# Repeated matmuls on the tensor engine in the waits of a four-stage convolution and attention kernel

## The chip, the cores and the metric

One core of a Trainium2 chip runs the whole kernel. The metric is the device time of one execution in microseconds; the median of three runs of the kernel before is 1879.36 us (1878.1 to 1879.47).

## The reference, cut to what matters

The input is x of 8 images, 64 channels, 56 by 56 pixels. Four residual blocks follow one another, each on a group-normalised x (32 groups of 2 channels, over all pixels of an image):

```python
x = x + _L0_conv_ref(_gn(x), ...)   # dynamic 3x3 filter: per channel cf times per pixel sf, 9 taps summed
x = x + _L1_conv_ref(_gn(x), ...)   # v * sigmoid(q . mean of k): two 64x64 products and a gate
x = x + _L2_conv_ref(_gn(x), ...)   # 3x3 convolution, 64 to 64 channels, weights -1, 0 or 1
x = x + _L3_conv_ref(_gn(x), ...)   # attention over all 3136 pixels: softmax(Q K) V, dk 16, dv 64
```

The mean and the variance of a group need the whole picture, so no stage can begin before the stage ahead of it has ended.

## The kernel before, in words

Two images lie side by side on the 128 partitions (64 channels each). So there are 4 groups of two images, worked off one after the other by `group(g, more)` on every engine; the first three in a loop, the last one unrolled behind it. A picture of 3136 pixels is cut into 7 chunks (NJ) of 448 pixels (CH, 8 rows). PSUM has 8 banks, PS[:, 0] to PS[:, 7]; `small` is bank 7, where the one-column results of the statistics go.

On the tensor engine a group runs as follows, in program order (nothing but this order and the semaphore waits sets when an instruction runs):

- The filter taps of block 0 (`taps`, L1085 and L1093), until the sums are in xw.
- `pair_stats(1)` (L1113, its two parts L1038 and L1042): DVE has gathered mean and variance per channel; a matmul by `pair` averages the means of the two channels of a group (`pair_mean`), DVE forms the squared difference, a second matmul averages that (`pair_var`), DVE adds epsilon (L483), POOL takes the power -0.5 (L954), DVE forms the bias (L487), and ACT normalises chunk by chunk (L777).
- For block 1 the engine then multiplies the pooled mean by wk (L1115), waits for DVE, multiplies by wq and half8 (L1117, L1118), waits until DVE has built U (L616), and does 7 times two fp32 matmuls of 448 columns (L1126, L1127).
- `pair_stats(2)` (L1130), and the convolution: per chunk 18 matmuls (L1135), the first of which waits until ACT has normalised two chunks.
- `pair_stats(3)` (L1145), and the 7 products with the joined weights of Q and K (L1148). ACT and DVE split them into three bf16 parts, and SP's DMAs spread them into Qa and Ka.
- The first maxima. `tile_of(bank, s, b, t)` (L1160 to L1164) is two matmuls of 64 output partitions and 448 columns each, one for each image (so a tile is a pair of matmuls). For the first superblock 49 tiles (TILES) are written to banks 0 to 6 in turn in the order FIRST_ORDER; DVE takes the maximum of each row (L672), and for the rows of three of the seven blocks ACT then sums the exponentials (L854). The tile that follows in the same bank waits for that (`first_used`, `first_summed`). Between them `value_columns` (L1156) makes the transposed values.
- DVE splits the maxima into bf16 parts (`split_max`, L679 to L688, `negm`). PE transposes these (`max_rows`, L1188), ACT copies them into Qa (L869, `mrow`), and only then can the scores begin (L1195).
- 7 superblocks of 25 steps each: scores (L1195), exponentials on ACT (L897), values (L1239), and the maxima of the next superblock (L1163 again, with L665 on DVE). In the last superblock of a group the front of the next group (statistics and filters of block 0) is laid between; these waits call `pair_mean` and `pair_var` themselves and not `pair_stats`.

The places that the change and the prediction touch are the two lines of `pair_stats`, the lines behind L1115 and L1118, and the loop L1273 to L1288.

Of the kernel before, what the change touches and what calls it, by code (L numbers as in the profile page):

```python
# [25 lines left out]
CH = ROWS * W  # L26
NJ = HW // CH
# [13 lines left out]
PITCH = 32  # L41
# [9 lines left out]
TILES = NJ * NJ  # L51
# [32 lines left out]
def order_first():  # L84

    blocks = [b for b in range(ACT_BLOCKS, NJ)]
    summed = {m * NJ // ACT_BLOCKS: m for m in range(ACT_BLOCKS)}
    row = [summed[n] if n in summed else blocks.pop(0) for n in range(NJ)]
    return [(b, t) for t in range(NJ) for b in row]


FIRST_ORDER = order_first()
# [76 lines left out]
def build(nc, x, weights, vectors, cst, out):  # L169
    with ExitStack() as ctx:  # L170
        def sb(name, shape, dt=F32):
            return ctx.enter_context(nc.sbuf_tensor(name, shape, dt))
# [15 lines left out]
        selb = sb("selb", [3 * PITCH, TAPS, P], BF16)  # L188
        identb = sb("identb", [P, P], BF16)
# [55 lines left out]
        PS = ctx.enter_context(nc.psum_tensor("PS", [P, 8, 512], F32))  # L245
# [8 lines left out]
        def pad_rows(t, r0, n, c0=0):  # L254

            return t[:, r0 * PW + c0:(r0 + n) * PW + c0].rearrange("p (r w) -> p r w", w=PW)[:, :, 0:W]
# [7 lines left out]
        def wcol(name):  # L264
            return wz[:, COLS[name][0]:COLS[name][1]]
# [761 lines left out]
        def _(pe):  # L1027
            mm = nc.tensor.matmul
# [7 lines left out]
            def pair_mean(g, layer, bank):  # L1036
                pe.wait_ge(gn_mean[layer], g + 1)
                mm(bank[:, 0:1], pair, mv[:, 0:1], start=True, stop=True).then_inc(gn_pm[layer], 1)  # L1038

            def pair_var(g, layer, bank):  # L1040
                pe.wait_ge(gn_sq[layer], g + 1)
                mm(bank[:, 1:2], pair, sq[:, :], start=True, stop=True).then_inc(gn_pv[layer], 1)  # L1042
# [31 lines left out]
                last.then_inc(sft_ready, 1)  # L1074

            def group(g, more):
                def pair_stats(layer):
                    pair_mean(g, layer, small)
                    pair_var(g, layer, small)

                def spread_tap(j, t):

                    k = NJ * g + j
                    pe.wait_ge(prod_ready, TAPS * k + t + 1)
                    mm(PS[:, t % TAP_BANKS, 0:CH], selb[:, t, :], SF[:, ds(j * CH, CH)],  # L1085
                       start=True, stop=True).then_inc(tap_ready, 1)
# [23 lines left out]
                add_tap(NJ - 1, 0, TAPS - 1)  # L1110


                pair_stats(1)  # L1113
                pe.wait_ge(pooled_ready, 2 * g + 2)
                mm(small[0:2 * CR, 20:21], wcol("wk"), pooled[:, 1:2], start=True, stop=True).then_inc(km_ps, 1)  # L1115
                pe.wait_ge(km_ready, g + 1)
                mm(small[:, 21:22], wcol("wq")[0:2 * CR], km[:, 0:1], start=True, stop=True)  # L1117
                mm(small[:, 22:23], half8[0:2 * CR], km[:, 1:2], start=True, stop=True).then_inc(u_ps, 1)  # L1118
                for j in range(NJ):
                    pe.wait_ge(xn_ready[1], NJ * g + j + 1)  # L1120
                    if j == 0:
                        pe.wait_ge(U_ready, g + 1)
                    if j >= 3:
                        pe.wait_ge(gated_ready, NJ * g + j - 2)
                    xnj = pad_rows(xnp, ROWS * j + 1, ROWS, 1)
                    mm(PS[:, j % 3, 0:CH], wcol("wv"), xnj, start=True, stop=True)  # L1126
                    mm(PS[:, 3 + j % 3, 0:CH], U[:, :], xnj, start=True, stop=True).then_inc(l1_ps, 1)  # L1127


                pair_stats(2)  # L1130
                def convolve(j, need):
                    for src, ready in ((xh, xh_ready), (xl, xl_ready)):
                        pe.wait_ge(ready, NJ * g + need)
                        for t in range(TAPS):
                            last = mm(PS[:, j, 0:CH], wt[:, t * P:(t + 1) * P],  # L1135
                                      pad_rows_at(src, j * (ROWS * PW) + (t // 3) * PW + t % 3, ROWS),
                                      start=(src is xh and t == 0), stop=(src is xl and t == TAPS - 1))
                    last.then_inc(conv_ready, 1)
# [3 lines left out]
                convolve(NJ - 1, NJ)  # L1142


                pair_stats(3)  # L1145
                for j in range(NJ):
                    pe.wait_ge(xn_ready[3], NJ * g + j + 1)
                    mm(PS[0:4 * DK, j, 0:CH], wcol("qk3"), xnf[:, j * CH:(j + 1) * CH],  # L1148
                       start=True, stop=True).then_inc(qk_ps, 1)
                def value_columns(i):  # L1150

                    if i:
                        pe.wait_ge(v_ready, NJ * g + i)
                    for j in range(4 * i, min(4 * i + 4, NQ)):
                        r = key_rows(j)
                        last = mm(PS[0:r, 7, (j % 4) * P:(j % 4 + 1) * P], xnf[:, j * QC:j * QC + r], wcol("wv3"),  # L1156
                                  start=True, stop=True)
                    last.then_inc(v_ps, 1)

                def tile_of(bank, s, b, t):  # L1160

                    for h in range(2):
                        last = mm(PS[C * h:C * h + C, bank, 0:CH], Qa[0:KROWS, h, s * CH + b * C:s * CH + b * C + C],  # L1163
                                  Ka[0:KROWS, h, t * CH:(t + 1) * CH], start=True, stop=True)  # L1164
                    return last
# [17 lines left out]
                def max_rows(sidx, bank):  # L1183

                    rowb = PS[:, bank, :].bitcast(BF16)
                    pe.wait_ge(negm, sidx + 1)
                    for b in range(NJ):
                        last = nc.tensor.transpose(rowb[KROWS:KROWS + 3, b * BLK:(b + 1) * BLK], mp[:, b, :], identb[:, :])  # L1188
                    last.then_inc(mrow_ps, 1)
# [80 lines left out]

                pe.wait_ge(q_first, 16 * (SPREADS * (g + 1) + 1))
                pe.wait_ge(k_first, 16 * (SPREADS * (g + 1) + 1))
                for i in range(TILES):  # L1273
                    b, t = FIRST_ORDER[i]
                    if i < NJ:
                        pe.wait_ge(rest_h, NJ * g + i + 1)
                    elif FIRST_ORDER[i - NJ][0] < ACT_BLOCKS:
                        pe.wait_ge(first_summed, ACT_TILES * g + sum(b < ACT_BLOCKS for b, _ in FIRST_ORDER[:i - NJ + 1]))
                    else:
                        pe.wait_ge(first_used, TILES * g + i - NJ + 1)  # L1280
                    if i == FIRST_KEYS * NJ:
                        pe.wait_ge(k_rest, 16 * (SPREADS * (g + 1) + 1))
                    tile_of(i % NJ, 0, b, t).then_inc(first_ready, 1)
                    if i % NJ == NJ // 2:
                        value_columns(i // NJ)
                pe.wait_ge(v_ready, NJ * (g + 1))
                max_rows(NJ * g, 7)
                pe.wait_ge(mrow, NJ * g + 1)  # L1288
                pe.wait_ge(q_rest, 16 * (SPREADS * (g + 1) + 1))
                for j in range(2):  # L1290
# [17 lines left out]
            with pe.Fori(0, GROUPS - 1) as g:  # L1308
                group(g, True)
            group(GROUPS - 1, False)  # L1310


# [64 lines left out]
```

## Time and profile before

| what | value |
|---|---|
| median of three runs | 1879.36 us |
| the profiled execution | 1879.96 us, of which the trace spans 1878.2 us |
| PE busy | 1646.5 us (88%) |
| DVE, ACT, POOL busy | 1258.0, 1249.8, 1099.3 us |
| mean granted clock of TensorE | 0.950 |

All times in the trace count from the start of its span. In a row, a bracket at the end says how long the engine was idle before the row and who released it. In a row of windows "(x12)" is the number of instructions, and PEclk is the granted clock of TensorE over the window: 1.00 is 2.4 GHz, 0.50 is 1.2 GHz, and a value between says that the window holds some of both. A group of two images takes some 460 us. The waits at issue lie in its first 150 us, and the first group's are shown in most rows.

### The profile page before, as it was taken

To read this page: it belongs to the slowest core of one execution; us is meant where nothing else is said; L and a number is where in the kernel's file an instruction comes from. 1 tells how busy PE (TensorE), PEld (TensorE's weight loads), DVE (VectorE), ACT (ScalarE), POOL (GpSimd) and SP (SyncE) were. 2 spreads that over 40 slices of the span, in tenths; PEclk is the share of its full clock that TensorE was granted. 3 is DMA by queue.
4 is the path that set the end of the run, shared out by engine and by line. 5 is a ranking of instruction groups with operands and counts; after the bars stand their busy time and mean duration, and the time that the engine had idled before them with its cause. 6 is when DMAs were issued, how large, how long until landed. Compare 5 with 4: busy or idle time off the path is not lost.

```text
span 1878.2 us, 35981 instructions
## 1 busy us (share of the span) xinstructions
PE 1646.5 (88%) x10840; PEld 826.0 (44%) x10840; DVE 1258.0 (67%) x2446; ACT 1249.8 (67%) x2324; POOL 1099.3 (59%) x898
## 2 busy tenths in 40 slices
PE   5887899999887699999988779999999787999997
PEld 4363344444436344444444534444454353444442
DVE  5947777775584777777467477777748657777760
ACT  2036788888412788888831278888872347888885
POOL 3610577778651067777855006777777402677777
PEclk9988899999889899999998889999999898999998
DMA  2004000000000400000000040000000011000000
GB/s 84 0 1 86 2 7 6 6 6 7 11 0 1 86 1 6 6 6 7 11 7 1 1 85 1 6 6 11 6 6 6 0 27 26 6 6 6 6 6 11
DMA packets 10104, 26.91 MB, mean 14 GB/s; under 512 B 2256, under 2 KB 6608, under 8 KB 9424
## 3 DMA queue, kind: packets, MB, share of 16 engines
q1 hardware_dynamic: 9936, 24.79, 5.5%
q8 instruction: 90, 1.47, 0.3%
q14 instruction: 78, 0.64, 0.1%
HBM read 8.73 MB, written 6.42 MB: 8 GB/s over the span
## 4 chain that ended last, share of the span: by engine, by line
PE 54%; issue 15%; DVE 12%; POOL 9%; ACT 9%; POOLq 1%; DVEq 0%; ACTq 0%
PE PS L1239 22%; PE PS L1163 11%; PE PS L1195 10%; DVE nmt L672 4%; ACT PS L854 3%; DVE nmt L665 2%; ACT Pb L897 2%; PE PS L1060 2%; POOL VT L970 2%; POOL VT L965 2%; PE PS L1135 2%; POOL VT L967 2%; POOL VT L974 1%; POOL accP L1008 1%; PE PS L1126 1%
## 5 line engine op out<-in xcount | busy, mean ns | idle before, releaser
L665 DVE TENSOR_REDUCE nmt<-PS 128x1 f32<-128x448 f32 x1176 | 680.3, 620 | 280.8 <-PE PS L1163 276.4
L1008 POOL TENSOR_TENSOR accP<-accP,Pb 128x512 f32<-128x512 f32 (+1 forms) x532 | 678.3, 1275 | 168.1 <-ACT Pb L897 144.6
L897 ACT ACTIVATE Pb<-PS 128x896 f32<-128x896 f32 (+1 forms) x700 | 638.9, 914 | 130.2 <-PE PS L1195 107.9
L1239 PE MATMUL PS<-Pb,VT 128*64 128x448 f32 x2800 | 656.0, 548 | 4.4 <-ACT Pb L897 3.6
L1163 PE MATMUL PS<-Ka,Qa 96*64 96x448 bf16 x2744 | 480.9, 362 | 55.9 <-DVE nmt L665 28.1
L1195 PE MATMUL PS<-Qa,Ka 99*64 99x448 bf16 x2744 | 489.8, 358 | 5.3 <-ACT Qa L869 4.0
L854 ACT ACTIVATE PS<-PS,nmt 128x448 f32<-128x448 f32 x588 | 356.3, 606 | 56.8 <-DVE nmt L672 29.4
L1163 PEld LDWEIGHTS PS<-Ka,Qa 96*64 96x64 bf16 x2744 | 159.4, 111 | 324.3 <-issue 127.2
L1195 PEld LDWEIGHTS PS<-Qa,Ka 99*64 99x64 bf16 x2744 | 162.3, 111 | 248.8 <-issue 184.3
L1239 PEld LDWEIGHTS PS<-Pb,VT 128*64 128x64 f32 x2800 | 191.6, 138 | 96.2 <-ACT Pb L897 24.5
L777 ACT ACTIVATE xnp<-xw,nb,rstd 128x448 f32<-128x448 f32 x56 | 40.5, 750 | 204.9 <-DVE nb L487 204.9
L1001 POOL TENSOR_TENSOR accQ<-Pb 128x512 f32<-128x512 f32 x28 | 35.6, 1271 | 234.2 <-ACT Pb L897 234.2
L579 DVE SCALAR_TENSOR_TENSOR Pb<-PS,cf,xnp 128x448 f32<-128x448 f32 x252 | 154.9, 677 | 17.1 <-PE PS L1085 13.4
L1093 PE MATMUL PS<-Pb,cs 128*128 128x448 f32 x280 | 135.5, 566 | 0.7 <-DVE Pb L579 0.7
L1008 POOL TENSOR_TENSOR accQ<-accQ,Pb 128x512 f32<-128x512 f32 x84 | 106.7, 1270 | 46.2 <-ACT Pb L897 44.9
L854 ACT ACTIVATION_READ_ACCUMULATOR PS<-PS,nmt 128x1 f32 x588 | 116.0, 197 | 0.0
L954 POOL TENSOR_TENSOR rstd<-ve,mhalf 128x1 f32<-128x1 f32 x16 | 8.8, 550 | 172.0 <-DVE ve L483 172.0
L672 DVE TENSOR_REDUCE nmt<-PS 128x1 f32<-128x448 f32 x196 | 104.8, 613 | 1.7 <-PE PS L1163 1.7
L1085 PE MATMUL PS<-xnf,selb 96*128 (+1 forms) x252 | 84.9, 376 | 13.3 <-issue 6.2
L777 ACT ACTIVATE xnf<-xw,nb,rstd 128x448 f32<-128x448 f32 x28 | 20.7, 752 | 102.8 <-DVE nb L487 102.8
L1135 PE MATMUL PS<-xh,wt 128*128 (+1 forms) x252 | 64.3, 404 | 10.6 <-ACT xh L777 10.6
L1085 PEld LDWEIGHTS PS<-xnf,selb 96*128 96x128 bf16 x252 | 25.0, 99 | 90.5 <-DVE Pb L579 50.7
(141 smaller groups left out, 1435.0 us busy)
## 6 DMA issues: line engine op xcount, KB each, us to landing
xin<-in_x SPq DMA_DIRECT2D x4, 1568.0 KB, 12.2
out<-xw SPq DMA_DIRECT2D x28, 224.0 KB, 1.9
Qa<-parts SPq DMA_DIRECT2D x24, 168.0 KB, 6.9
Ka<-parts SPq DMA_DIRECT2D x24, 112.0 KB, 3.8
Ka<-parts SPq DMA_DIRECT2D x24, 84.0 KB, 2.6
wz<-in_weights SPq DMA_DIRECT2D x1, 829.0 KB, 8.2
Qa<-parts SPq DMA_DIRECT2D x24, 28.0 KB, 1.9
cs<-in_cst SPq DMA_DIRECT2D x1, 576.0 KB, 8.8
```

The source lines that it names most:

```text
L579: nc.vector.scalar_tensor_tensor(out=rows(prod[:, t, :]), in0=rows(PS[:, t % TAP_BANKS, 0:CH]), scalar=cf[:, t:t + 1], in1=pad_rows_at(xnp ...
L665: nc.vector.reduce_max(nmt[:, target % 2, b, t:t + 1], PS[0:BLK, bank, 0:CH], X, negate=True).then_inc(mx_free, 1)
L672: nc.vector.reduce_max(nmt[:, 0, b, t:t + 1], PS[0:BLK, i % NJ, 0:CH], X, negate=True).then_inc(first_used, 1)
L854: return nc.scalar.activation(PS[0:BLK, bank, 0:CH], PS[0:BLK, bank, 0:CH], ACT.Exp, bias=nmt[:, target % 2, b, t:t + 1], accum_out=sm[:, ...
L897: nc.scalar.activation(Pb[0:r, j % PSLOTS, :, :], PS[0:r, 2 * (k % 2):2 * (k % 2) + 2, 0:CH], ACT.Exp).then_inc(exp_done, 1)
L1008: nc.gpsimd.tensor_tensor((accQ if j < TO_ACCP else accP)[0:r, :, REST:CH], (accQ if j <= TO_ACCP else accP)[0:r, :, REST:CH], Pb[0:r, j % ...
L1085: mm(PS[:, t % TAP_BANKS, 0:CH], selb[:, t, :], SF[:, ds(j * CH, CH)], start=True, stop=True).then_inc(tap_ready, 1)
L1093: mm(PS[:, ACCB + odd, 0:CH], identf, prod[:, t, :], start=(t == 0), stop=(t == TAPS - 1)).then_inc(tap_added, 1)
L1135: last = mm(PS[:, j, 0:CH], wt[:, t * P:(t + 1) * P], pad_rows_at(src, j * (ROWS * PW) + (t // 3) * PW + t % 3, ROWS), start=(src is xh an ...
L1163: last = mm(PS[C * h:C * h + C, bank, 0:CH], Qa[0:KROWS, h, s * CH + b * C:s * CH + b * C + C], Ka[0:KROWS, h, t * CH:(t + 1) * CH], start ...
L1195: ins = mm(PS[c:c + C, 2 * (k % 2) + h, 0:CH], Ka[0:KROWS + 3, h, j * QC + c:j * QC + c + C], Qa[0:KROWS + 3, h, s * CH:(s + 1) * CH], sta ...
L1239: last = mm(PS[C * h:C * h + C, OB, 0:CH], VT[:, j, C * h:C * h + C], Pb[:, j % PSLOTS, h, :], start=(j == 0), stop=(j == NQ - 1))
```

## The change

`pair_stats` gets a second argument, and a new function `keep_busy(n)` issues n matmuls of 96 rows, 128 output partitions and 448 columns in bf16 on constants, into bank 6. One stands between `pair_mean` and `pair_var` at each of the three places; behind `pair_var` stand 2, 6 and 5. Two more places in block 1 get 1 and 2. The loop over the first maxima goes on for 7 more turns, in each of which the engine waits until the bank is free and then issues a last tile again twice (its result is overwritten later and never read), and 4 more such tiles stand behind `max_rows`. No other engine's program changes.

```diff
             def group(g, more):
-                def pair_stats(layer):
+                def keep_busy(n):
+
+                    for _ in range(n):
+                        mm(PS[:, 6, 0:CH], identb[0:3 * PITCH, :],
+                           selb[:, :, :].rearrange("p t c -> p (t c)")[:, 0:CH], start=True, stop=True)
+
+                def pair_stats(layer, meanwhile):
                     pair_mean(g, layer, small)
+                    keep_busy(1)
                     pair_var(g, layer, small)
+                    keep_busy(meanwhile)
...
-                pair_stats(1)
+                pair_stats(1, 2)
                 pe.wait_ge(pooled_ready, 2 * g + 2)
                 mm(small[0:2 * CR, 20:21], wcol("wk"), pooled[:, 1:2], start=True, stop=True).then_inc(km_ps, 1)
+                keep_busy(1)
                 pe.wait_ge(km_ready, g + 1)
                 mm(small[:, 21:22], wcol("wq")[0:2 * CR], km[:, 0:1], start=True, stop=True)
                 mm(small[:, 22:23], half8[0:2 * CR], km[:, 1:2], start=True, stop=True).then_inc(u_ps, 1)
+                keep_busy(2)
...
-                pair_stats(2)
+                pair_stats(2, 6)
...
-                pair_stats(3)
+                pair_stats(3, 5)
...
-                for i in range(TILES):
-                    b, t = FIRST_ORDER[i]
+                for i in range(TILES + NJ):
                     if i < NJ:
                         pe.wait_ge(rest_h, NJ * g + i + 1)
                     elif FIRST_ORDER[i - NJ][0] < ACT_BLOCKS:
                         pe.wait_ge(first_summed, ACT_TILES * g + sum(b < ACT_BLOCKS for b, _ in FIRST_ORDER[:i - NJ + 1]))
                     else:
                         pe.wait_ge(first_used, TILES * g + i - NJ + 1)
+                    if i >= TILES:
+                        for _ in range(2):
+                            tile_of(i % NJ, 0, NJ - 1, NJ - 1)
+                        continue
+                    b, t = FIRST_ORDER[i]
...
                 max_rows(NJ * g, 7)
+                for _ in range(4):
+                    tile_of(NJ - 1, 0, NJ - 1, NJ - 1)
                 pe.wait_ge(mrow, NJ * g + 1)
```

## Rows read from the trace of the kernel before

**Rows 1.** The page: engine shares, and TensorE's clock in 40 slices
```profile
PE 1646.5 (88%) x10840; PEld 826.0 (44%) x10840; DVE 1258.0 (67%) x2446; ACT 1249.8 (67%) x2324; POOL 1099.3 (59%) x898
...
PEclk9988899999889899999998889999999898999998
```
**Rows 2.** Windows: start:end and length us, each engine's busy us, PEclk, DMA
```profile
90.98:96.10 5.12, 2.39 (x10) 2.08 (x11) 1.50 (x9) 2.39 (x4) 0.55 (x1) 0.50 0.01 2
96.10:99.72 3.62, 3.62 (x5) 1.82 (x6) 0.00 (x0) 0.58 (x2) 0.00 (x0) 0.50 0.00 0
116.47:120.20 3.73, 3.73 (x10) 3.34 (x11) 1.88 (x3) 3.73 (x7) 0.00 (x0) 0.50 0.02 4
```
**Rows 3.** Timeline, what ends each wait: start, length us, engine, line
```profile
93.79 0.21 PE L1115 MATMUL PS<-pooled,wz 128*16 128x1 f32 x2 [1.14 <-DVE pooled L610]
94.43 0.58 PE L1117 MATMUL PS<-km,wz 16*128 16x1 f32 x2 [0.42 <-DVE km L613]
96.10 1.83 PE L1126 MATMUL PS<-xnp,wz 128*128 128x448 f32 x2 [0.67 <-DVE U L616]
97.73 1.70 PE L1127 MATMUL PS<-xnp,U 128*128 128x448 f32 x2
97.73 0.34 PEld L1127 LDWEIGHTS PS<-xnp,U 128*128 128x128 f32 x1 [0.41 <-issue]
116.47 3.72 PE L1135 MATMUL PS<-xh,wt 128*128 x9 [2.65 <-ACT xh L777]
150.67 4.29 PE L1148 MATMUL PS<-xnf,wz 128*64 128x448 f32 x6 [2.10 <-ACT xnf L777]
```
**Rows 4.** Timeline, from the last first maxima to the first scores
```profile
183.41 6.99 DVE L672 TENSOR_REDUCE nmt<-PS 128x1 f32<-128x448 f32 x13
187.19 0.73 PE L1163 MATMUL PS<-Ka,Qa 96*64 96x448 bf16 x5
191.19 0.18 DVE L688 TENSOR_REDUCE mp<-nm 128x7 bf16<-128x21 f32 x1
191.51 0.91 PE L1188 MATMUL PS<-identb,mp 128*3 128x128 bf16 x7 [3.59 <-DVE mp L688]
192.46 0.91 ACT L869 ACTIVATE Qa<-PS 3x896 bf16<-3x896 bf16 x1 [2.20 <-PE PS L1188]
193.42 1.70 PE L1195 MATMUL PS<-Qa,Ka 99*64 99x448 bf16 x8 [1.00 <-ACT Qa L869]
```
**Rows 5.** Windows around the same place, in all four groups
```profile
172.00:187.90 15.90, 11.93 (x96) 7.12 (x96) 15.90 (x31) 11.30 (x30) 0.00 (x0) 1.00 0.54 131
187.95:191.50 3.55, 0.00 (x0) 0.01 (x1) 3.32 (x11) 1.63 (x6) 0.00 (x0) 0.57 0.00 0
191.50:198.70 7.20, 5.84 (x29) 2.62 (x31) 1.78 (x3) 4.98 (x10) 1.97 (x2) 0.50 0.01 2
652.50:662.92 10.42, 9.08 (x43) 3.94 (x45) 2.39 (x4) 5.58 (x12) 2.53 (x2) 0.50 0.01 2
1116.11:1123.72 7.61, 6.27 (x31) 2.85 (x33) 1.78 (x3) 5.41 (x11) 2.39 (x2) 0.50 0.01 2
1573.40:1581.10 7.70, 6.43 (x31) 2.83 (x33) 1.78 (x3) 5.46 (x11) 2.53 (x2) 0.50 0.01 3
656.46:659.50 3.04, 3.04 (x14) 1.44 (x16) 1.78 (x3) 2.91 (x8) 1.78 (x2) 0.50 0.00 0
168.00:171.40 3.40, 3.40 (x20) 2.20 (x21) 2.87 (x7) 2.07 (x6) 0.00 (x0) 0.50 1.07 127
```
**Rows 6.** Timeline: neighbouring pairs of 448 columns at either clock
```profile
195.47 0.59 PE L1195 MATMUL PS<-Qa,Ka 99*64 99x448 bf16 x2 [0.35 <-ACT Pb L897]
195.84 0.59 PE L1163 MATMUL PS<-Ka,Qa 96*64 96x448 bf16 x2
...
199.53 0.36 PE L1195 MATMUL PS<-Qa,Ka 99*64 99x448 bf16 x2
199.72 0.36 PE L1163 MATMUL PS<-Ka,Qa 96*64 96x448 bf16 x2
```

## The prediction

> **What bounds the kernel now.** I read the page first. PE is busy 88% of the span and the other engines 67% or less, so PE is the engine to look at; but its clock is at tenths of 8 and 9 in a good part of the slices [rows 1]. The mean granted clock is 0.950; with two levels, 1.00 and 0.50, that is 10% of the span, some 188 us, at 1.2 GHz. A slow clock costs only where PE itself is what the others wait for, and then half of the busy time in it. So the second look is at windows cut at the waits, with the clock in them, and the third at the timeline inside.
>
> In each group the clock falls in the same places. Around the first statistics it is 0.50 from the pair mean at 90.98, with PE busy 2.39 of 5.12 us on one-column matmuls and weight loads, and it stays there over the next 3.62 us of unbroken fp32 work [rows 2]. At the second statistics PE waits 2.65 us for ACT, and then convolves 3.73 us at 0.50 [rows 2, 3]. At the third it waits 2.10 us [rows 3]. The costliest place is the end of the first maxima: PE does nothing from 187.95 to 191.50, the clock falls in it (mean 0.57), and the 7.20 us that follow run at 0.50 [rows 5]. All this lies on the path: the next stage cannot begin before a mean, a maximum or the split of it is there.
>
> What makes the clock return is seen in the same rows: each time PE had worked without a break for over 3 us (96.10 to 99.72, 116.47 to 120.20). 3.04 us without a break, from 656.46, were not enough, and the clock stayed at half until 662.92 [rows 2, 5].
>
> What keeps it up is seen from 172.00 to 187.90: PE busy 11.93 of 15.90 us, with a break in each row of tiles, and the clock stayed at 1.00 throughout [rows 5].
>
> **The repeats behind the first maxima.** A tile is one pair of 448-column matmuls. Pairs start 0.37 us apart at 0.50 (195.47, 195.84) and 0.19 us apart at 1.00 (199.53, 199.72) [rows 6]. The change adds 7 x 2 = 14 pairs before `max_rows`: 2.6 us at the full clock, 5.2 us at half. DVE's maxima come every 6.99 / 13 = 0.54 us and end at 183.41 + 6.99 = 190.40; each frees a bank for two pairs (0.37 us). So at the full clock PE keeps pace with DVE, and the last two pairs end near 190.45 + 0.75 = 191.2 at the latest. The split maxima come at 191.19 + 0.18 = 191.37 and PE's transposes began at 191.51 [rows 4]. Nothing is late: the added work lies under DVE's maxima and splits, and costs 0. If the clock has fallen first, 14 pairs from 187.95 end at 193.1, 1.6 us late, less if it returns on the way.
>
> Behind `max_rows` come 4 pairs, 0.75 us at full clock and 1.5 us at half, in the 1.00 us in which PE waits for ACT's copy (0.91 us) [rows 4]: cost 0, or 0.5 us at half clock.
>
> Does the clock stay? PE worked until 187.19 + 0.73 = 187.9 [rows 4]. The repeats begin at about 188.0, the first bank being free, and from there to 191.2 PE has 2.6 us of work in 3.3, about the share that held the clock from 172.00 to 187.90. After that come the transposes, the 4 pairs and the scores; the thinnest place is from the scores to the end of the first exponential, under 1 us. I take it as staying up, with one group in four where it falls all the same, since the last row of tiles has a break just before 187.
>
> What is then saved is half of the busy time that PE now has at 0.50: 5.84, 9.08, 6.27 and 6.43 us in the four groups [rows 5], together 27.6, half 13.8 us. That it is PE that ends the steps there: of the 7.20 us it is busy 5.84, and the rest is the ACT copy and the first exponential, which do not get faster. The half holds for streaming and less for the fixed part of each. For this and for the one group in four in which the clock falls or the repeats come late by up to 1.6 us, I take off 1.5: -12.3 us. Bounds: 0 (the clock falls anyway) and -13.8.
>
> **keep_busy.** It is one matmul of 448 columns in bf16, so by the pairs 0.19 or 0.37 us, and here the clock is mostly at half already when it begins.
> - First statistics. The clock has fallen before the pair mean, where no repeat is; nothing is saved until it returns. The repeats are 1, 2, 1, 2 in waits of 0.50 (L1042, as long as the rows' others of this kind), 1.14, 0.42 and 0.67 us [rows 3]: 0.37, 0.75, 0.37 and 0.75 us at half clock. The last is 0.08 us too long, the one at L1117 leaves 0.05. PE still pauses between them, so the clock returns when it does now, after some 3.5 us of the fp32 work from 96.10. Value taken: +0.1 us a group. Bounds: +0.5 (one 0.37 us matmul more than a wait holds, and a bit) and -1.8 (half of the 3.62 us).
> - Second statistics. 6 x 0.37 = 2.2 us stand in 2.65 us [rows 3]. That leaves 0.4 us of pause ahead of the convolution. If it counts as a break, the clock returns 3.7 us into the convolution as now; if not, up to 2.6 us sooner, worth 1.3 us. Value taken: 0. Bounds: +0.1 and -1.9 a group (half of 3.73).
> - Third statistics. 5 x 0.37 = 1.9 us in 2.10 us. The six matmuls from 150.67 take 4.29 us, so the first product (two of them) takes 1.4 us where 0.7 would do [rows 3]; ACT waits for that one alone, since then it has more to do than PE. Value 0, bounds +0.1 and -0.7.
>
> These three give +0.4 us over four groups, with bounds of +2.8 and -17.6.
>
> The Trainium skill speaks against these repeats: TensorE: Matmul & The Clock Gate, Part 3, "The mechanism", has it that a weight load goes beside a running matmul only where the row groups differ. By that rule each fp32 weight load behind a repeat would wait for its end; an estimate from this and the loads' 0.34 us at half clock is three loads in the first statistics and one in each other one, up to 5 x 0.34 x 4 = 6.8 us, and the sum would be -5 us. The trace does not agree: the L1127 load of 0.34 us, on all 128 rows, begins at 97.73, while PE is busy without a break from 96.10 to 99.72 with matmuls on all rows [rows 2, 3]. So I leave it at the sum above.
>
> **Sum.** -12.3 + 0.4 = -11.9. The profiled execution took 1879.96 us (its span 1878.2 and 1.8 around it); this gives 1868.1. The median of the runs is 0.6 lower: 1867.5 us. What is late next in the freed place is ACT's exponential and then PE at its full speed.
>
> **The rivals.**
> 1. The clock also returns sooner, or from the first matmul, in the stages behind the statistics. For it: the repeats turn waits of 2.65 and 2.10 us into almost unbroken work. Against: the pauses left are 0.2 to 0.4 us, and unbroken work of 3.04 us was not enough [rows 5]. Price: half of 3.73 and half of 3.62 us and 0.7 us a group, four times 4.4 = 17.6 at most; I take 15 of it: 1852 us.
> 2. The clock falls all the same behind the maxima or in the copy of `max_rows`, and what is saved in one step is paid in the next. For it: the break before 187, the transposes, which are short, and ACT's 0.91 us. Against: the share of work above. Price: some 3 of the 13.8 us remain: 1876 us, and within 0.2% of before.
> 3. Slower. The clock falls at about 188.5 as now and the repeats run at half clock: they end 1.6 us late, the 4 behind `max_rows` 0.5 us late, and the clock is not given back before the scores; +2.1 us a group, +8.4, with +2.8 from the statistics at their upper bounds: 1891 us. It decides if a repeat on half the output columns does nothing for the clock. Against it: from 168.00 to 171.40, at 0.50, PE did just such tiles and value columns without a break, and from 172.00 it is at 1.00 [rows 5]. 14 pairs at half clock are themselves such a stretch.
> 4. The change does not do what it says: the repeats leave clock and times as they are. That would be 1880 us; rival 2 holds this chance.
>
> The Trainium skill, in the same page, Part 4, has a rule for rival 2: a transpose does not count as PE activity as another matmul does. No row cited here shows it; the 0.91 us of transposes would then be a pause.
>
> **How the numbers follow.** The forecast, the maxima alone: 0.57. Rival 1: 0.17. Rival 2 with 4: 0.16. Rival 3: 0.10. A change under 0.2% (3.8 us) can't be told from none. Faster by more than that: 0.57 + 0.17 and a part of rival 2, 0.06: 0.80. Within: 0.11 (the rest of rival 2 and a mild rival 3). Slower: 0.09. The range goes down to rival 1, with 1851, and up to 1878 through rival 2.
>
> **What would show it.** In the profile after, the stretch from the last maximum to the third exponential at 1.00 in most groups, the transposes starting no later behind L688 than 0.14 us, and scores 0.19 us apart. The convolution's and L1126's first 3.5 us still at 0.50. Mean clock up from 0.950 to about 0.965. The forecast is wrong if the clock is at 0.50 behind the repeats, if the transposes start late, or if the first fp32 products of a stage run at 1.00.

## The result and the profile after

The changed kernel takes 1865.64 us (median of four runs, 1865.11 to 1866.51) against 1879.41 us of the kernel before (1878.1 to 1880.94): the ratio is 0.9928 with a 95% interval of 0.9913 to 0.9944. The forecast was 1867.5 us. The profiled executions are 1866.14 us and 1879.96 us, so 13.8 us less.

The page of the changed kernel, its engine shares and the clock in 40 slices, beside [rows 1]:

```profile
PE 1674.4 (90%) x11060; PEld 831.4 (45%) x11060; DVE 1258.4 (67%) x2446; ACT 1248.1 (67%) x2324; POOL 1096.4 (59%) x898
...
PEclk9988999999889899999989899999999899999999
```

PE has 220 matmul records more and is busy 28 us longer, in a shorter span; the other engines do what they did. The mean granted clock went from 0.950 to 0.964.

The timeline from the last row of tiles to the first scores answers to [rows 4] (line numbers are 10 higher behind the change: L1173 is the tile, L1198 the transposes, L1205 the scores):

```profile
186.36 4.29 PE L1173 MATMUL PS<-Ka,Qa 96*64 96x448 bf16 x33
...
190.36 0.18 DVE L688 TENSOR_REDUCE mp<-nm 128x7 bf16<-128x21 f32 x1
...
190.69 0.55 PE L1198 MATMUL PS<-identb,mp 128*3 128x128 bf16 x7
191.17 0.95 PE L1173 MATMUL PS<-Ka,Qa 96*64 96x448 bf16 x8
191.28 0.91 ACT L869 ACTIVATE Qa<-PS 3x896 bf16<-3x896 bf16 x1 [1.85 <-PE PS L1198]
192.24 0.95 PE L1205 MATMUL PS<-Qa,Ka 99*64 99x448 bf16 x8
```

The 14 repeated pairs run on from the last real ones and end at 190.65. The last split maximum ends at 190.54 and the transposes begin 0.15 us later, where it was 0.14 before. They take 0.55 us and not 0.91, and the scores 0.95 and not 1.70.

The windows of the changed kernel: a stretch of each statistics and what follows, the repeats, and then, in each of the four groups, from the first transpose to the start of the sixth exponential (columns as in [rows 2]):

```profile
90.69:95.40 4.71, 4.05 (x16) 1.99 (x17) 1.50 (x9) 2.39 (x4) 0.55 (x1) 0.62 0.01 2
95.40:98.68 3.28, 3.28 (x6) 1.64 (x6) 0.00 (x0) 0.32 (x1) 0.00 (x0) 0.50 0.00 0
115.64:119.16 3.52, 3.52 (x10) 3.13 (x11) 1.88 (x3) 3.52 (x6) 0.00 (x0) 0.50 0.00 0
149.75:153.30 3.55, 3.55 (x5) 1.03 (x6) 0.62 (x1) 2.05 (x4) 0.00 (x0) 0.50 0.00 0
186.36:190.65 4.29, 3.95 (x36) 1.55 (x32) 4.08 (x13) 2.33 (x7) 0.00 (x0) 1.00 0.02 4
190.69:200.09 9.40, 8.57 (x73) 4.17 (x75) 3.74 (x7) 7.67 (x15) 4.05 (x4) 1.00 0.00 2
650.83:660.23 9.40, 8.57 (x73) 4.19 (x75) 3.74 (x7) 7.67 (x15) 4.04 (x4) 1.00 0.00 1
1108.36:1117.77 9.41, 8.58 (x73) 4.20 (x75) 3.75 (x7) 7.67 (x16) 4.05 (x4) 1.00 0.00 1
1562.32:1571.56 9.24, 8.49 (x73) 4.09 (x75) 3.66 (x7) 7.59 (x15) 4.05 (x4) 1.00 0.01 3
```

The same four stretches of the kernel before, first transpose to sixth exponential:

```profile
191.51:203.24 11.73, 10.38 (x65) 4.80 (x67) 3.84 (x7) 7.86 (x16) 4.06 (x4) 0.69 0.01 3
652.50:665.81 13.31, 11.97 (x65) 5.32 (x67) 3.93 (x7) 7.97 (x15) 4.06 (x4) 0.61 0.01 2
1116.11:1128.04 11.93, 10.59 (x65) 4.90 (x67) 3.84 (x7) 7.87 (x16) 4.05 (x4) 0.68 0.01 2
1573.40:1585.26 11.86, 10.59 (x65) 4.80 (x67) 3.76 (x7) 7.91 (x16) 4.05 (x4) 0.68 0.01 2
```

Read the length and PEclk. Before, 48.83 us at 0.61 to 0.69; after, 37.45 us at 1.00 in every group. That is 11.4 of the 13.8 us. The other 2.4 us are spread over all stretches; the largest piece, 1.2 us in the sum of the four groups, lies between the first pair mean and the second. In the stages behind the statistics the first 3.3 to 3.6 us still run at 0.50, in the convolution and in the Q and K products as in the fp32 work of block 1.

### The profile page after: what moved, and what is told of

Same layout as the page of the kernel before. It is cut to its first block, busy times and chain, and to the rows that moved or that the text cites. A ratio compares the mean times of both kernels' runs of the same rounds, so it can differ in the third digit from the quotient of the medians.

```text
span 1864.3 us, 36442 instructions
## 1 busy us (share of the span) xinstructions
PE 1674.4 (90%) x11060; PEld 831.4 (45%) x11060; DVE 1258.4 (67%) x2446; ACT 1248.1 (67%) x2324; POOL 1096.4 (59%) x898
## 4 chain that ended last, share of the span: by engine, by line
PE 52%; issue 15%; DVE 12%; POOL 10%; ACT 9%; POOLq 1%; DVEq 0%; ACTq 0%
PE PS L1249 21%; PE PS L1173 11%; PE PS L1205 10%; DVE nmt L672 4%; ACT PS L854 3%; ACT Pb L897 3%; DVE nmt L665 3%; POOL accP L1008 2%; POOL VT L965 2%; POOL VT L970 2%; POOL VT L967 2%; PE PS L1060 2%; PE PS L1145 2%; POOL VT L974 1%; PE PS L1136 1%
## 5 line engine op out<-in xcount | busy, mean ns | idle before, releaser
L1173 PE MATMUL PS<-Ka,Qa 96*64 96x448 bf16 x2888 | 493.6, 359 | 57.0 <-DVE nmt L665 28.1
L1205 PE MATMUL PS<-Qa,Ka 99*64 99x448 bf16 x2744 | 485.0, 354 | 3.3 <-ACT Pb L897 2.8
L1173 PEld LDWEIGHTS PS<-Ka,Qa 96*64 96x64 bf16 x2888 | 164.8, 110 | 332.5 <-issue 123.2
L1205 PEld LDWEIGHTS PS<-Qa,Ka 99*64 99x64 bf16 x2744 | 161.0, 110 | 245.6 <-issue 182.9
L579 DVE SCALAR_TENSOR_TENSOR Pb<-PS,cf,xnp 128x448 f32<-128x448 f32 x252 | 154.7, 677 | 15.3 <-PE PS L1093 13.8
L1093 PE MATMUL PS<-xnf,selb 96*128 (+1 forms) x252 | 83.6, 370 | 13.8 <-issue 6.9
## 6 DMA issues: line engine op xcount, KB each, us to landing
xin<-in_x SPq DMA_DIRECT2D x4, 1568.0 KB, 11.8
```

What stands on the lines that cost most here:

```text
L579: nc.vector.scalar_tensor_tensor(out=rows(prod[:, t, :]), in0=rows(PS[:, t % TAP_BANKS, 0:CH]), scalar=cf[:, t:t + 1], in1=pad_rows_at(xnp ...
L1205: ins = mm(PS[c:c + C, 2 * (k % 2) + h, 0:CH], Ka[0:KROWS + 3, h, j * QC + c:j * QC + c + C], Qa[0:KROWS + 3, h, s * CH:(s + 1) * CH], sta ...
```

## The experiments

My theory: the gain is the clock behind the first maxima, and keep_busy gives almost nothing, because the clock has fallen before it begins (that reason holds in part only, see below). The rival: keep_busy carries a good part. All ratios are to the kernel before on the same chip.

**maxima_only**, without keep_busy:

```diff
-                    keep_busy(1)
                     pair_var(g, layer, small)
-                    keep_busy(meanwhile)
```

and without the two calls in block 1.

> Only the repeats behind the first maxima (7 x 2 tiles and the 4 behind max_rows); no keep_busy. My theory, that these carry the gain and keep_busy nearly none: 1866 to 1868 us. If keep_busy carried the gain: 1877 to 1880 us. From the comparison of the traces of before and after (in the first fp32 stage the sum of four groups is 1.2 us shorter, from the last split maximum to the sixth exponential 11.3 us) I expect 1867 us.

1867.74 us, ratio 0.9951 (0.9937 to 0.9964).

**statistics_only**, keep_busy alone:

```diff
-                for i in range(TILES + NJ):
+                for i in range(TILES):
...
-                for _ in range(4):
-                    tile_of(NJ - 1, 0, NJ - 1, NJ - 1)
```

> Only keep_busy at the three statistics and in block 1; nothing behind the maxima. My theory: 1878 to 1880 us, the same as before within 0.2%, since a clock that has fallen before the mean returns only after unbroken work. The rival, that the clock returns sooner in these stages: 1872 us or less.

1877.26 us, ratio 0.9998 (0.9989 to 1.0007). keep_busy as it stands gives nothing that can be measured, and costs nothing. That the whole is 2 us faster than maxima_only may be chance: the two intervals overlap. In the profile of the whole, the stretch from the first pair mean to the second is 0.6 and 0.8 us shorter in two groups, 0.2 shorter in one and 0.4 longer in one. In the sum of the groups this stretch takes 84.5 us there, 85.7 us before, and 86.5 us in maxima_only and in statistics_only alike, so it does not follow keep_busy alone.

**fourteen_only** and **four_only** take the repeats behind the maxima apart; neither has keep_busy.

```diff
 # fourteen_only
-                for _ in range(4):
-                    tile_of(NJ - 1, 0, NJ - 1, NJ - 1)
 # four_only
-                for i in range(TILES + NJ):
+                for i in range(TILES):
```

> Only the 7 x 2 tiles between the last first maximum and max_rows; neither the 4 tiles behind max_rows nor keep_busy. If the clock is held up by the 14 tiles and the 4 are not needed: 1867 us and clock 1.00 up to the third exponential. If the wait for ACT's copy (1.0 us), with few matmuls on either side of it, lets the clock fall: in some groups 0.50 again behind the scores, 1868 to 1874 us.

> Only the 4 tiles behind max_rows. By my theory the clock has fallen by then, the 4 tiles take 1.5 us at half clock in a wait of 1.0 us and delay the scores by up to 0.5 us a group, and may bring the clock back one step sooner: 1875 to 1881 us. If they alone gave the gain: 1867 us.

fourteen_only: 1871.98 us, ratio 0.9971 (0.9962 to 0.9980); four_only: 1877.56 us, 1.0004 (0.9994 to 1.0013). The 4 are nothing by themselves. Without them the 14 give less by the medians, 1871.98 us against 1867.74 us of maxima_only on the same chip; the two intervals just touch, but every run of fourteen_only (1870.03 to 1875.86) is slower than every run of maxima_only (1867.66 to 1868.21). In fourteen_only's timeline of the second group PE waits 1.00 us for the copy and 0.71 us for the exponential, and the clock falls at 653.82:

```profile
650.08 0.55 PE L1194 MATMUL PS<-identb,mp 128*3 128x128 bf16 x7
651.63 0.95 PE L1201 MATMUL PS<-Qa,Ka 99*64 99x448 bf16 x8 [1.00 <-ACT Qa L869]
653.29 0.38 PE L1201 MATMUL PS<-Qa,Ka 99*64 99x448 bf16 x2 [0.71 <-ACT Pb L897]
...
654.68 2.95 PE L1245 MATMUL PS<-Pb,VT 128*64 128x448 f32 x8
```

Its window shows the half clock:

```profile
653.82:657.24 3.42, 3.42 (x16) 1.28 (x12) 1.78 (x3) 2.82 (x9) 2.53 (x2) 0.50 0.00 0
```

The 8 value matmuls take 2.95 us, where the changed kernel's take 1.67 us in the first group. The third group has such a fall too, the first and the last have none: this is rival 2's mechanism, in half of the groups.

**one_tile_a_turn**, **four_tiles_a_turn** and **transposes_a_turn** change only what each of the 7 turns does:

```diff
-                        for _ in range(2):
+                        for _ in range(1):    # one_tile_a_turn; range(4) in four_tiles_a_turn
                             tile_of(i % NJ, 0, NJ - 1, NJ - 1)
...
-                        for _ in range(2):    # transposes_a_turn
-                            tile_of(i % NJ, 0, NJ - 1, NJ - 1)
+                        for _ in range(7):
+                            nc.tensor.transpose(PS[:, i % NJ, :].bitcast(BF16)[:, 0:P], identb[:, :], identb[:, :])
```

> As the changed kernel, but each of the 7 turns issues one tile and not two. PE is then busy 0.19 of each 0.54 us between DVE's maxima. If what counts is that there is no pause longer than about half a microsecond: 1866 us, as with two. If what counts is how much PE works: the clock falls in the wait for the maxima as before, 1870 to 1879 us.

> As the changed kernel, but each of the 7 turns issues four tiles and not two: 28 pairs x 0.19 = 5.2 us from about 188.0, so they end near 193.1 where the transposes could begin at 191.5: 1.6 to 1.7 us late a group at full clock, 1872 to 1873 us. This is the price of repeats that outlast their wait (the mechanism of the slower rival). If added tiles cost nothing even then: 1866 us.

> As the changed kernel, but each of the 7 turns issues 7 bf16 transposes of 128 columns (some 0.4 us) and not two tiles (0.37 us). If a transpose counts for the clock as a matmul does: 1866 us and clock 1.00 behind the maxima. If it does not, as the Trainium skill has it (TensorE: Matmul & The Clock Gate, Part 4): the clock falls in the wait for the maxima as before, 1870 to 1879 us.

One tile: 1875.03 us, 0.9985 (0.9976 to 0.9994). Four: 1874.37 us, 0.9977 (0.9967 to 0.9987). Transposes: 1865.67 us, 0.9933 (0.9917 to 0.9948), as the changed kernel.

The windows of one_tile_a_turn, over the last tiles with the repeats and behind them:

```profile
184.50:188.83 4.33, 2.64 (x23) 0.97 (x20) 4.08 (x13) 2.33 (x7) 0.00 (x0) 1.00 0.01 4
188.83:196.08 7.25, 6.90 (x37) 3.05 (x39) 1.78 (x3) 4.97 (x10) 1.96 (x2) 0.53 0.00 0
```

and those of transposes_a_turn:

```profile
185.89:189.36 3.47, 3.25 (x49) 2.75 (x50) 3.24 (x11) 1.61 (x5) 0.00 (x0) 1.00 0.00 0
189.38:198.80 9.42, 8.59 (x73) 4.21 (x75) 3.76 (x7) 7.69 (x16) 4.09 (x4) 1.00 0.01 3
```

With one tile PE was busy 2.64 of 4.33 us, without a pause over 0.6 us, and the clock fell in all four groups; with two it was 3.95 of 4.29 us, and stayed. In both kernels PE had paused 0.98 us just before, ahead of the value columns (L1166). So it is not the length of the longest pause alone. With 49 transposes in place of the 14 pairs the clock stays just as well.

Four tiles show the price of repeats that outlast the wait. Its transposes and its last split maximum:

```profile
190.77 0.18 DVE L688 TENSOR_REDUCE mp<-nm 128x7 bf16<-128x21 f32 x1
...
193.03 0.55 PE L1198 MATMUL PS<-identb,mp 128*3 128x128 bf16 x7
```

They begin 2.08 us behind the split and not 0.15: 1.9 us late, four times 7.7, and 1865.6 + 7.7 = 1873.3 us against 1874.4 measured (1.6 to 1.7 us a group and 1872 to 1873 us were expected). It is rival 3's mechanism, at full clock.

**ahead_of_mean** fills the waits from their start, while the clock is still up, and the ones behind more fully, as at full clock more repeats fit:

```diff
-                def pair_stats(layer, meanwhile):
+                def pair_stats(layer, meanwhile, ahead, bank=6):
+                    keep_busy(ahead, bank)
                     pair_mean(g, layer, small)
-                    keep_busy(1)
+                    keep_busy(2)
...
-                pair_stats(1, 2)
+                pair_stats(1, 5, 16)
...
-                pair_stats(2, 6)
+                pair_stats(2, 12, 17)
...
-                pair_stats(3, 5)
+                pe.wait_ge(l2_done, NJ * g + 1)
+                pair_stats(3, 9, 10, 0)
```

with 2 and 3 in place of 1 and 2 in block 1. The third takes bank 0 and waits until that is free, since bank 6 still holds the last chunk of the convolution.

> The changed kernel with repeats also where PE waits for DVE's statistics ahead of each pair mean, before the clock falls: 16, 17 and 10 of keep_busy in waits of 3.59, 3.70 and 2.22 us (3.0, 3.2, 1.9 us at full clock), and more of them in the waits behind (2 between mean and variance; then 5, 12 and 9; in block 1 2 and 3). My theory, that the loss is half of PE's busy time at half clock and the clock holds if the waits are filled from their start: 4 x (1.8 + 1.9 + 0.7 + 0.3 for faster one-column matmuls) = 18.8 us less: 1847 to 1850 us, mean clock above 0.98. The rival, that one-column matmuls and short pauses let it fall anyway, or that repeats at half clock outlast their waits: 1862 us or more.

1846.18 us, ratio 0.9833 (0.9819 to 0.9846), mean clock 0.987. Against the changed kernel's 0.9928 that is 18 us less (19.5 by the medians, which were not taken together); 18.8 was expected, and a time just above the measured one, 1847 to 1850 us. Its timeline around the first two statistics:

```profile
86.41 3.19 PE L1080 MATMUL PS<-selb,identb 96*128 96x448 bf16 x16
90.16 0.38 PE L1038 MATMUL PS<-mv,cs 128*128 128x1 f32 x2 [0.56 <-DVE mv L473]
...
94.45 0.99 PE L1137 MATMUL PS<-xnp,wz 128*128 128x448 f32 x2
...
105.11 3.38 PE L1080 MATMUL PS<-selb,identb 96*128 96x448 bf16 x17
108.96 0.38 PE L1038 MATMUL PS<-mv,cs 128*128 128x1 f32 x2 [0.47 <-DVE mv L473]
...
110.09 2.43 PE L1080 MATMUL PS<-selb,identb 96*128 96x448 bf16 x12
112.87 2.15 PE L1146 MATMUL PS<-xh,wt 128*128 x9 [0.35 <-ACT xh L777]
114.86 2.08 PE L1146 MATMUL PS<-xl,wt 128*128 x9
```

The waits are there, shorter by what is filled, and nothing is late. The first 9 matmuls of the convolution take 2.15 us where they took 3.72 [rows 3], and from the first mean to U's product there are 94.45 - 90.16 = 4.29 us where there were 5.12 [rows 2]. Against the trace of the changed kernel the sum of four groups is 9.3 us shorter from the first mean to the second, 6.8 us from the second to the third, and 4.4 us from the third to the transposes. Those 20.5 us are as much as the two profiled executions differ by.

**long_without_ahead** and **ahead_alone** take this apart:

```diff
 # long_without_ahead: the first repeats away
-                pair_stats(1, 5, 16)
+                pair_stats(1, 5, 0)
...
 # ahead_alone: all others away
-                    keep_busy(2)
                     pair_var(g, layer, small)
-                    keep_busy(meanwhile)
```

and in ahead_alone also without the two calls in block 1.

> As ahead_of_mean but with no repeat ahead of the pair means; those behind stay (2 between mean and variance, then 5, 12 and 9, in block 1 2 and 3). The clock then falls around each mean as in the changed kernel, and at half clock 12 repeats take 4.5 us in a wait of 2.65, 9 take 3.4 in 2.1, 5 take 1.9 in 1.14. My theory: about 2 to 4 us late a group, less up to 2 us where the longer unbroken work brings the clock back sooner: 1868 to 1878 us, slower than the changed kernel. If the repeats behind the mean carried ahead_of_mean's gain: 1850 us or less.

> As ahead_of_mean but with only the repeats ahead of the pair means (16, 17, 10), none between mean and variance, behind the variance or in block 1. If the first long wait is what lets the clock fall: 1846 to 1850 us. If the waits behind (2.65 and 2.10 us ahead of the convolution and of the Q and K products, a row of short ones in block 1) let it fall all the same: 1855 to 1866 us, with 0.50 in the convolution.

long_without_ahead: 1872.70 us, 0.9968 (0.9955 to 0.9982); ahead_alone: 1862.72 us, 0.9912 (0.9896 to 0.9928). The first lies in the range of my theory, the second in the range for the case that the waits behind let the clock fall. Without the first repeats the same 12 run at half clock and outlast the wait; in long_without_ahead's timeline (its profiled execution was the slowest of its five, 1877.8 us) the convolution begins 5.3 us behind the mean (112.53) and not 4.1:

```profile
112.53 0.38 PE L1038 MATMUL PS<-mv,cs 128*128 128x1 f32 x2 [3.69 <-DVE mv L473]
...
113.68 4.64 PE L1080 MATMUL PS<-selb,identb 96*128 96x448 bf16 x12
117.81 3.40 PE L1146 MATMUL PS<-xh,wt 128*128 x9
```

A window of it, from the first of the 12 on: PE works without a break for 6.7 us, and all of it at half clock.

```profile
113.68:120.40 6.72, 6.72 (x21) 3.98 (x21) 2.37 (x6) 5.53 (x9) 0.55 (x1) 0.50 0.00 0
```

With the first repeats alone the clock holds at the mean and falls in the wait behind it; windows of ahead_alone, the last 1.6 us of that wait and the convolution after it:

```profile
113.98:115.60 1.62, 0.00 (x0) 0.01 (x1) 0.00 (x0) 1.58 (x3) 0.00 (x0) 0.50 0.00 0
115.60:120.80 5.20, 5.20 (x14) 4.64 (x15) 2.64 (x5) 5.20 (x9) 0.00 (x0) 0.50 0.00 0
```

So each wait of a chain needs its own filling, and neither half has the whole: 1862.7 and 1872.7 us alone, 1846.2 together.

**group_end_too** adds repeats where PE waits between two groups:

```diff
                 denominators(NJ * g + NJ - 1, 7)
+                if more:
+                    keep_busy(14, 3)
```

> ahead_of_mean with 14 more repeats (2.6 us) at the end of each of the first three groups, where PE waits 3.09 us and the first taps of the next group then run at 0.50 for some 5 us. If PE ends the steps there: up to 3 x 2.4 = 7 us less, 1839 to 1843 us. If DVE's products end them, or the repeats hold up the step into the next group: 1845 to 1849 us, no change.

1848.26 us, ratio 0.9839 (0.9825 to 0.9853), no different from ahead_of_mean, and in the range for the case that PE does not end the steps there. The place, in the timeline of ahead_of_mean and then of this kernel:

```profile
489.66 0.64 PE L1221 MATMUL PS<-accP,ones 128*64 128x256 f32 x4
...
493.40 1.19 PE L1094 MATMUL PS<-xnf,selb 96*128 96x448 bf16 x3 [3.09 <-issue]
...
495.28 0.55 PE L1094 MATMUL PS<-xnf,selb 96*128 96x448 bf16 x1 [0.69 <-DVE Pb L579]
```

```profile
491.86 0.65 PE L1221 MATMUL PS<-accP,ones 128*64 128x256 f32 x4
492.44 2.82 PE L1080 MATMUL PS<-selb,identb 96*128 96x448 bf16 x14
495.72 0.74 PE L1094 MATMUL PS<-xnf,selb 96*128 96x448 bf16 x3 [0.45 <-issue]
497.47 0.36 PE L1094 MATMUL PS<-xnf,selb 96*128 96x448 bf16 x1 [1.01 <-DVE Pb L579]
```

The wait was filled (0.45 us left of 3.09), the first taps run at full clock (0.74 us for three and not 1.19), and the taps then wait 1.01 us for DVE where they waited 0.69. From the denominators to the first tap it is 3.9 us with the repeats, 3.7 without. PE does not end the steps here, so its clock buys little.

## Why the prediction was right

**The repeats behind the maxima.** Forecast -12.3 us, between 0 and -13.8; measured -11.4 us in the four stretches of the trace. maxima_only has -11.0 us as the difference of medians, and -9.2 us (-6.8 to -11.8) by its ratio. The steps held as they were put: the repeats keep pace with DVE's 0.54 us and end before the split (190.65, forecast "near 191.2" with a split 0.8 us later; that forecast took 0.75 us for the last two pairs, which are 0.37 us at full clock), the transposes begin at 0.15 us, the 4 fit into ACT's copy, the clock is 1.00. The size is near, but by an offset. I took 1.5 us off for a group in which the clock falls, and none fell in the profile. In its place the half was too much: in the first group PE's busy time in the stretch, without the 0.88 us that the 4 added pairs take behind the transposes, fell from 10.38 to 8.57 - 0.88 = 7.69 us, 2.7 us, near what was worked out (half of 5.84 is 2.9). The stretch fell by 2.3 us only, since what PE does not spend on its own work in it grew by the rest. Half the slow busy time was an upper bound here.

That the sum came within 2 us of the measured time is in part luck: the term that was worked out was 0.9 us too large by the trace, and 2.4 us came from places for which the prediction had +0.4 us.

**Does the clock stay?** The prediction argued from 2.6 us of work in 3.3 us; the trace has 3.95 us in 4.29 us, and the clock stayed in all four groups. fourteen_only and one_tile_a_turn show how near a fall was: with less work, it fell in two and in four of the groups. So rival 2 was a real danger at 0.16. The prediction also took it that the clock returns after some 3.5 us of unbroken work. That is no rule: in long_without_ahead 6.7 us of it did not, and in the kernel before the clock was still at 0.50 just before 662.92, 6.4 us into the unbroken work from 656.46 [rows 5].

**keep_busy.** Forecast +0.4 us; statistics_only measured a ratio of 0.9998 +- 0.0009, so -0.4 us, within +-1.7. The value was right, and the reason given for it was not. The prediction says that the clock is mostly at half already when the repeats begin, and at the first statistics since before the pair mean. In the trace of the changed kernel the clock has fallen before the mean in 2 of the 12 statistics; in the other 10 it falls 0.2 to 1.2 us behind the start of the mean, in nine of them after the first repeat has begun. In the kernel before it falls behind the start of the mean in 8 of 12, but at the first statistics before it in all four groups. The second statistics of the first group, timeline and windows:

```profile
111.53 0.38 PE L1038 MATMUL PS<-mv,cs 128*128 128x1 f32 x2 [3.69 <-DVE mv L473]
111.77 0.35 PE L1080 MATMUL PS<-selb,identb 96*128 96x448 bf16 x1
...
112.86 2.40 PE L1080 MATMUL PS<-selb,identb 96*128 96x448 bf16 x6
115.64 3.68 PE L1145 MATMUL PS<-xh,wt 128*128 x9 [0.38 <-ACT xh L777]
```

```profile
111.53:112.30 0.77, 0.59 (x3) 0.31 (x3) 0.32 (x2) 0.00 (x0) 0.00 (x0) 1.00 0.00 0
112.35:115.64 3.29, 2.85 (x8) 1.17 (x9) 0.33 (x3) 1.59 (x3) 0.55 (x1) 0.50 0.00 0
```

The first repeat ran at 1.00 and the clock fell all the same, behind the 3.69 us in which PE had nothing to do. ahead_of_mean puts work into that wait, and more behind it, and none of the 12 falls is left. The pause that was to keep the clock down is there (0.38 us ahead of the convolution, 0.4 forecast), and the convolution's first 3.52 us ran at 0.50. That this pause is what kept it down is not shown: in long_without_ahead there is no such pause, and the clock stayed down too. The cost in block 1 is less than the +0.1 us a group: in the two groups in which the clock was down through the whole wait, mean to U's product took 5.12 and 5.13 us as before (5.12).

**The weight loads.** The estimate by the Trainium skill (TensorE: Matmul & The Clock Gate, Part 3) was 6.8 us of loads that would stand behind the repeats. It took the page's row-group rule alone, though the same section of the Trainium skill also lets a load into the background weight buffer go ahead of running matmuls. The 0.9998 of statistics_only leaves no room for the 6.8 us, unless a gain of the same size hid them, and from the first pair mean to U's product the groups of the changed kernel take 4.71 to 5.13 us, and took 5.12 or 5.13 us before. The trace before was the better guide.

**The transposes.** The rule of the Trainium skill that a transpose does not count as PE activity (TensorE: Matmul & The Clock Gate, Part 4) stood beside rival 2. transposes_a_turn contradicts it: 49 transposes, busy 3.25 of 3.47 us, kept the clock at 1.00 in this kernel, at 1865.67 us.

**Rival 1** needed a clock in the stages behind the statistics that returns sooner, or is up from their first matmul. For this change statistics_only refutes both. With the waits filled from their start the second comes true: ahead_of_mean has it, and its 18 us are about the 17.6 us that the rival's price had as its top (they hold some gains that the price did not count, as the waits of block 1).

What stays open: whether the 2.1 us between the changed kernel and maxima_only are more than chance, and by what rule the clock counts. A profile shows one execution of each kernel, so in how many groups the clock falls may differ in others; the runs of fourteen_only spread over 5.8 us, those of maxima_only over 0.6.

## What to carry to other kernels

Look for the granted clock behind each wait of TensorE, and take half of PE's busy time at half clock as an upper bound of what filler matmuls can bring there (here 13.8 us, and 11.4 us came). Filler has to begin when the wait begins, and fill every wait of the chain. Begun behind a wait of 2.2 to 3.7 us that stood empty it brought nothing here, even where the clock was still up at its first matmul, and sized for the full clock it then outlasted the wait. Size it from the producer's pace (here 0.37 us in 0.54), and leave it out where another engine ends the steps.

## What was not expected of the hardware

Transposes by TensorE held the clock as well as matmuls. A busy row without any pause above 0.6 us (2.64 of 4.33 us, one tile a turn) did not: the clock fell in all four groups. The clock fell in a chain whose first wait was filled but whose next, of 2.64 us, was not. And a fall need not come within the pause, or late in it: behind the maxima of the kernel before it came about 0.5 us after PE had stopped (mean 0.57 over the 3.55 us from 187.95 [rows 5]), at the statistics mostly after PE had begun to work again.
